# Stores issued from ScalarE's queue in a batched Gram-matrix kernel

## The reference

```python
Z = jnp.einsum('bnd,bmd->bnm', inputs, inputs)
n = inputs.shape[1]
li, lj = jnp.tril_indices(n, k=-1)
return Z[:, li, lj]
```

## Time and profile before

| | |
|---|---|
| median of three runs | 437.03 us |
| profiled execution, its own time | 437.67 us |
| its span (first to last instruction) | 435.9 us |
| PE busy | 385.4 us (88%) |
| DVE busy | 363.7 us (83%) |
| POOL busy | 197.2 us (45%) |
| ACT busy | 179.3 us (41%) |
| DMA, mean over the span | 346 GB/s |
| read from HBM, written to it | 134.22 MB, 16.52 MB |

### The profile page before, as it was taken

The page is one execution under the profiler, slowest core; times in us unless marked ns, Lnnn a source line. Parts: engine busy times, 40 slices in busy tenths (PEclk is TensorE's granted clock), DMA queues, the critical chain, the costliest instruction groups (busy, mean ns, idle before and its releaser), DMA issues.

```text
span 435.9 us, 68822 instructions
## 1 busy us (share of the span) xinstructions
PE 385.4 (88%) x33024; PEld 377.5 (87%) x33024; DVE 363.7 (83%) x224; ACT 179.3 (41%) x834; POOL 197.2 (45%) x980
## 2 busy tenths in 40 slices
PE   4569999999999999999998999989899998989810
PEld 4569999999999999999998989989899998989810
DVE  5248899999999999897997979799697979979734
ACT  0101125454444535354444544533445454345372
POOL 0000082745628174471817446281744628173584
PEclk9999999999999999999999999999899999999965
DMA  5589999999999999999999999999999999999416
GB/s 199 192 312 388 387 387 387 387 391 392 387 398 386 402 387 368 369 394 357 356 398 344 390 377 387 353 352 378 373 384 368 379 365 373 361 386 368 107 34 156
DMA packets 72378, 151.01 MB, mean 346 GB/s; under 512 B 4640, under 2 KB 4768, under 8 KB 72352
## 3 DMA queue, kind: packets, MB, share of 16 engines
q1 hardware_dynamic: 72352, 150.75, 95.3%
HBM read 134.22 MB, written 16.52 MB: 346 GB/s over the span
## 4 chain that ended last, share of the span: by engine, by line
PE 35%; DMA 28%; DVE 16%; SPq 10%; issue 6%; POOL 3%; ACT 0%; DVEq 0%; POOLq 0%
PE bank_set L256 35%; DMA x_in<-x_dram 25%; DVE x_turned L203 12%; SPq L138 9%; DVE row_halves L219 3%; DMA y_dram<-packed_rows 3%; POOL packed_rows L122 3%; DVE packed_rows L122 1%; DVE x_turned L225 0%; SPq L145 0%; ACT packed_rows L117 0%; ACT products L282 0%; DVEq L202 0%; DVEq L218 0%; DVEq L64 0%
## 5 line engine op out<-in xcount | busy, mean ns | idle before, releaser
L256 PE MATMUL bank_set<-x_turned 32*64 32x64 f32 x33024 | 385.4, 237 | 30.0 <-issue 12.1
L256 PEld LDWEIGHTS bank_set<-x_turned 32*64 32x64 f32 x33024 | 377.5, 132 | 37.8 <-issue 21.9
L203 DVE STREAM_TRANSPOSE x_turned<-x_in 128x2048 f32<-128x2048 f32 x128 | 290.6, 2286 | 58.0 <-DMA x_in<-x_dram 41.5
L122 POOL COPY packed_rows<-row_halves 32x60 f32<-32x60 f32 (+30 forms) x961 | 194.9, 204 | 232.3 <-DMA y_dram<-packed_rows 132.5
L282 ACT COPY products<-bank_set 128x768 f32<-128x768 f32 (+2 forms) x96 | 69.0, 729 | 215.4 <-PE bank_set L256 204.9
L219 DVE STREAM_TRANSPOSE row_halves<-products 128x1024 f32<-128x1024 f32 x64 | 76.8, 1203 | 6.9 <-POOL packed_rows L122 5.0
L117 ACT COPY packed_rows<-row_halves 128x128 f32<-128x128 f32 x256 | 56.4, 300 | 17.4 <-DMA y_dram<-packed_rows 15.9
L111 ACT COPY packed_rows<-row_halves 128x32 f32<-128x32 f32 (+30 forms) x481 | 62.3, 220 | 0.0
L282 ACT ACT_TABLE_LOAD x1 | 1.3, 1283 | 15.8 <-PE bank_set L256 15.8
L122 DVE COPY packed_rows<-row_halves 32x2 f32<-32x2 f32 (+30 forms) x31 | 3.5, 191 | 0.0
L225 DVE MEMSET x_turned<- 128x2048 f32 x1 | 1.8, 1765 | 1.2 <-PEq L325 1.2
## 6 DMA issues: line engine op xcount, KB each, us to landing
x_in<-x_dram SPq DMA_DIRECT2D x256, 512.0 KB, 10.8
y_dram<-packed_rows SPq DMA_DIRECT2D x30, 504.0 KB, 9.6
y_dram<-packed_rows SPq DMA_DIRECT2D x2, 380.0 KB, 3.9
y_dram<-packed_rows SPq DMA_DIRECT2D x2, 124.0 KB, 3.9
```

Of the source, the lines that this page charges most:

```text
L122: return copy(packed_rows[first:first + BLOCK, group % 2, :, at + BLOCK:at + i], row_halves[first + BLOCK:first + HALF, i, :, 0:i - BLOCK])
L203: nc.vector.transpose(x_turned[:, j].rearrange("p k c (i r) -> p k r c i", r=JOINED), x_in[:, k].rearrange("p k (r c d) -> p k r c d", r=J ...
L256: done = nc.tensor.matmul(bank_sets[s][side * HALF:(side + 1) * HALF, g, at, :], rows, rows, start=c == 0, stop=c == CHUNKS - 1)
```

## The change

The stores of groups 0 to 14 are issued from ScalarE's program, on its own DMA queue. SP issues the loads without them, and at the end the two pieces of group 15 as before. `store` is the same code with the issuing engine as a parameter, and `STORE_LAG` is gone. In ScalarE's main loop the stores of a group stand behind the first eviction that comes after the group's last packing, and ahead of the next group's packing. The stores of group 14 stand between the packing of groups 14 and 15, behind the last eviction. The waits are those that SP had, for `packed_home`, which ScalarE itself raises, and `packed_across`.

```diff
-    STORE_LAG = PIECE_LAG + 2 * PIECES + 3 + IN_RING
...
+        def store(engine, group, columns):
+            for side in range(SIDES):
+                first = group * GROUP + side * KEPT
+                engine.dma_start(y[first:first + KEPT, columns].rearrange("(h q) c -> q h c", q=BLOCK),
+                                 packed_rows[side * HALF:side * HALF + BLOCK, group % 2, :, columns]).then_inc(
+                    stored[group % 2], 16)
...
             for t in range(TILES):
                 load(t)
-                group, behind = divmod(t - STORE_LAG, GROUP_TILES)
-                if group >= 0 and behind == 0:
-                    store_whole(group)
-            for group in range((TILES - 1 - STORE_LAG) // GROUP_TILES + 1, GROUPS - 1):
-                store_whole(group)
...
+            def store_whole(group):
+                act.wait_ge(packed_home, (group + 1) * PIECES)
+                act.wait_ge(packed_across, (group + 1) * LONG_PIECES)
+                store(act, group, slice(0, PACKED))
+
             n = 0
+            stores = 0
             for lap in range(LAPS):
                 for s in range(SETS):
                     keep(lap, s)
+                    if n >= (stores + 1) * PIECES * 4:
+                        store_whole(stores)
+                        stores += 1
                     while n + PACK_LAG < (lap * SETS + s + 1) * SET_SLOTS - BLANK * SLOTS:
                         pack(n)
                         n += 1
 
             for n in range(n, (GROUPS * PIECES - 1) * 4):
+                if n == (GROUPS - 1) * PIECES * 4:
+                    store_whole(GROUPS - 2)
                 pack(n)
```

More of the change, by code:

```diff
@@ L165, in _ @@
             sync.wait_ge(last_carried, 1)
-            store(group, slice(long_rows, PACKED))
+            store(sync, group, slice(long_rows, PACKED))
             sync.wait_ge(packed_home, GROUPS * PIECES - 1)
             sync.wait_ge(last_packed, 1)
-            store(group, slice(0, long_rows))
+            store(sync, group, slice(0, long_rows))
             for b in range(2):
```

## The result

The changed kernel takes 433.5 us (median of 6 runs, 432.21 to 435.69) against 436.98 us for the kernel before on the same chip: ratio 0.9922, 95% interval 0.9901 to 0.9943, 3.5 us faster. A second series gave 433.48 us, ratio 0.9918 (0.9896 to 0.9939). The forecast was 425.6 us, a gain of 11.4 us. The sign was right, and most of that gain did not come.

What follows compares the result with a forecast made beforehand. Loads were taken to bound the last 60%, at 25.3 us a group against PE's 23.7. Span 435.9 - 8.7 - 3.3 + 0.5 = 424.4 us, then + 1.8 - 0.6 gave 425.6 us; range 421 to 441.

Steps and rivals of the forecast that it cites:

- What bounds the kernel: Last 60% of the kernel: loads set 25.3 us a group against PE's 23.7, with a few DMA engines late.
- The stores on a queue of their own: Load stream: a group's store costs loads 2.9 us instead of 3.6, so the period is 24.6 us.
- the same engines, the same rate: Rival, chance 0.30: engines stay as late, period 25.3 us, only the tail gains; run about 437 us.
- From period to time: Over 12.5 groups, less a 9.3 us lead of the loads: PE's end comes 8.7 us earlier.
- The tail: After the last evictions: an earlier store of group 12 frees POOL sooner; the end comes 3.3 us earlier.
- Store 13 against the last load: End of the load stream: this store cuts in on a load still on the way, costing 0.5 us.
- ScalarE: Its two added store issues a group take 1.8 us and cost PE nothing; its waits cost 0.
- The bound of 5.2 us: ScalarE's store issues up to 5.2 us a group cost PE nothing; above that each us costs one.

Runs made afterwards that it cites:

- e6: Changed kernel without the stores of groups 0 to 11 (that output is left out): 425.59 us, 0.9722 of the kernel before.
- e15: Changed kernel, groups 0 to 12 store only 16 of each side's 32 partitions (rest left out): 425.38 us, 0.9741 of the kernel before.
- e16: Changed kernel, groups 0 to 12 store only 18 of each side's 32 partitions (rest left out): 432.35 us, 0.9892 of the kernel before.
- e1: Changed kernel, but SP issues the stores of groups 0 to 11 at their old places, ScalarE only those of 12 to 14: 434.81 us.
- e10: Changed kernel with each store cut in four column parts, 8 DMAs a group: 435.0 us, 0.9961 of the kernel before.
- e13: Changed kernel, stores of groups 0 to 12 in four column parts, groups 13 to 15 whole: 429.42 us, 0.9827 of the kernel before.
- e14: Changed kernel, stores of groups 0 to 12 in four column parts, side 1 one eviction behind side 0: 428.19 us.
- e11: Kernel before, all stores on SP two tiles sooner and cut in two column halves: 438.86 us, 1.0044 of the kernel before.
- e2: Changed kernel, but SP issues the stores of groups 12 to 14 at their old places, ScalarE those of 0 to 11: 436.06 us.

## Why the prediction was wrong

*What bounds the kernel: right.* The loads give periods of 25.3 us, PE gives 23.7, and a part of the engines is late; e6 and e15 show both sides.

*The stores on a queue of their own: wrong, and this is the step that failed.* I took a cost of 2.9 us a store, near the byte bound, because all engines would start on a store together and loads would fill the gaps. Measured it is 25.4 - 21.7 = 3.7 us, what it was on SP's queue (3.6). A store does land sooner (6.6 us after its issue in the median, before 9.6), but one engine falls behind with its share of it (e15 and e16), and it does so on either queue. I had seen the spread of the landings and read it as an effect of the queue's order. The rival *the same engines, the same rate*, which I gave 0.30, is what happened; its 437 us was 3.5 too high.

*From period to time.* 8.7 us were to come off PE's end; the last eviction moved by 0.3 us the other way. PE's start was a second term, which I had put at nothing: in this execution its stalls there took 5.7 us more, so by this sum PE's end could have come only 10.7 - 5.7 = 5 us sooner even without any wait for loads (in e6, where such waits are nearly gone, its last eviction came 6.0 us sooner). With the period unchanged the late start cost nothing. It gave the loads a larger lead, and past the start DVE first waited for them at 268 us instead of 182.

*The tail: right in kind, a little small.* The forecast had ScalarE's end at 427.4 and the last 5.2 us behind it, 3.3 us gained. ScalarE ended at 425.37 + 2.20 = 427.6 and 4.3 us followed. By e1 this part is worth 2.2 us in the median, by both profiles 4.3.

*Store 13 against the last load.* Taken at 0.5 us, in the rival at 2 to 4; it was 0. It went out at 407.14, when only the late engine still had loads, and DVE was not yet free for it. This is why the rival's time was too high.

*ScalarE: right.* A pair of issues takes 0.81 us, not 1.8, and nothing waits for it. The bound of 5.2 us, under which issues were to cost nothing, holds only in mid-stream: in e10 3.7 us a group cost nothing to be seen there, and in the tail they counted in full.

*The Trainium skill*, "DMA: Bandwidth & Descriptors", section "Issuing engines are not separate DMA queues", says that DMAs of all issuers share the same 16 engines and that a second issuer saves only issue time. The period agrees, 25.4 us on two queues and 25.3 on one. What e13 and e14 add is that the same bytes cost less in shorter packets and smaller bursts.

*Open.* Which engine is late and why; why shorter packets ease it on ScalarE's queue and not on SP's (e11); and the 1.0 us that the early stores bring in e2.

## What to carry to other kernels

In these runs a transfer was as long as its last engine. Where the spread between first and last landing grows, ask for one engine's share before the bytes: a queue of its own frees a store from what is in front of it, not from that. A store that is worth moving is one for which someone waits at the end, and every DMA issue put on a working engine should be kept out of the tail.

## What the runs showed of the hardware that I had not expected

One of 16 DMA engines ran up to 6 us behind the others, with whole stores on either queue (in e1, whose early stores are SP's, the loads still run at 25 GB/s from 406 to 408 us); loads alone left it on time (1.6 us of spread in e6). Cutting 8064 B packets in four, with the two sides issued half a lap (4.45 us) apart, took 5.3 us off a kernel that moves the same bytes, though one engine still ran about 5 us behind at its end.
